# Mixing of two expert outputs on TensorE: diagonal products in place of scale, add and turn

## The reference

```python
scores = jax.nn.softmax(xf @ gate_w.T, axis=-1)
top_v, top_i = jax.lax.top_k(scores, TOP_K)              # TOP_K = 2
top_v = top_v / jnp.sum(top_v, axis=-1, keepdims=True)
for e in range(N_EXPERTS):                               # 8
    w_e = jnp.sum(jnp.where(top_i == e, top_v, 0.0), axis=-1)
    h = _gelu(xf @ fc1_w[e].T + fc1_b[e])
    y = h @ fc2_w[e].T + fc2_b[e]
    out = out + w_e[:, None] * y
shared = _gelu(xf @ w1_w.T + w1_b) * (xf @ w3_w.T + w3_b) @ w2_w.T + w2_b
return (out + shared)                                    # and x + this
```

## Time and profile before

| | us |
|---|---|
| median of 3 runs | 1638.67 |
| lowest and highest of them | 1627.11, 1644.32 |
| the profiled execution, its time | 1633.87 |
| its span in the trace | 1631.9 |
| busy in the span: PE, PEld, DVE, ACT, POOL | 1389.5, 1186.8, 1112.7, 770.3, 415.2 |

### The profile page before, as it was taken

How to read it: one execution, slowest core, us unless ns; L and a number is a source line. 1 busy time by engine, 2 the same in 40 slices (tenths; PEclk the granted TensorE clock), 3 DMA queues, 4 the chain that set the end, 5 groups by cost and what they waited for, 6 DMA issues and landing times. The chain is left out here.

```text
span 1631.9 us, 49725 instructions
## 1 busy us (share of the span) xinstructions
PE 1389.5 (85%) x19283; PEld 1186.8 (73%) x19283; DVE 1112.7 (68%) x3948; ACT 770.3 (47%) x1702; POOL 415.2 (25%) x686
## 2 busy tenths in 40 slices
PE   3858888888887679999995889989998869899998
PEld 3847777777776568778874657768887458777885
DVE  7867777777777864768766693644443774677764
ACT  3733333333334465656633432645555255556651
POOL 2732222222222701000022310356655041000003
PEclk9955555555555789999996579989999579999996
DMA  3000000000000246887966402423222555789865
GB/s 96 1 21 4 4 4 4 4 4 4 4 4 4 88 144 138 248 247 203 177 140 181 135 15 97 151 94 94 87 87 75 153 157 145 180 268 242 184 132 123
DMA packets 73124, 169.05 MB, mean 104 GB/s; under 512 B 18466, under 2 KB 43754, under 8 KB 70396
## 3 DMA queue, kind: packets, MB, share of 16 engines
q1 hardware_dynamic: 67516, 153.03, 35.5%
q0 software_dynamic: 5376, 12.85, 2.6%
HBM read 93.60 MB, written 67.42 MB: 99 GB/s over the span
## 5 line engine op out<-in xcount | busy, mean ns | idle before, releaser
L514 PE MATMUL gru_ps_r<-gru_hp,gru_wp 128*128 128x16 f16 x3920 | 199.7, 176 | 68.3 <-DVE gru_hp L489 68.3
L1375 DVE TENSOR_REDUCE l_mt<-l_ps 98x2 fp32r<-98x392 f32 x384 | 198.8, 560 | 72.7 <-PE l_ps L1139 70.1
L514 PEld LDWEIGHTS gru_ps_r<-gru_hp,gru_wp 128*128 128x128 f16 x3920 | 150.5, 105 | 88.7 <-DVE gru_hp L489 88.7
L1327 ACT ACTIVATE l_arena<-l_ps 98x784 f32<-98x784 f32 x192 | 158.3, 824 | 90.3 <-PE l_ps L1162 87.0
L514 PE MATMUL gru_ps_n<-gru_hp,gru_wp 128*128 128x16 f16 x3920 | 191.2, 174 | 0.0
L580 ACT ACTIVATE gru_reset<-gru_ps_r,gru_unscale 128x32 f32<-128x32 f32 x196 | 56.5, 288 | 216.6 <-PE gru_ps_r L514 216.6
L514 PEld LDWEIGHTS gru_ps_n<-gru_hp,gru_wp 128*128 128x128 f16 x3920 | 150.0, 104 | 0.0
L567 POOL TENSOR_TENSOR gru_kept<-gru_keep,l0s_state 128x32 f32<-128x32 f32 x196 | 49.4, 252 | 305.3 <-ACT gru_keep L582 305.3
L1139 PE MATMUL l_ps<-l_arena,l_arena 128*98 128x196 f32 x768 | 109.2, 262 | 5.8 <-DVE l_arena L1357 2.7
L1139 PEld LDWEIGHTS l_ps<-l_arena,l_arena 128*98 128x98 f32 x768 | 88.6, 166 | 27.4 <-DVE l_mt L1375 20.8
L1162 PE MATMUL l_ps<-l_unit,l_mt 98*98 98x196 f32 x768 | 103.0, 256 | 0.0
(11 more groups left out here) (390 smaller groups left out, 4033.0 us busy)
## 6 DMA issues: line engine op xcount, KB each, us to landing
l_arena<-qk SPq DMA_DIRECT2D x96, 294.0 KB
qk<-l_arena SPq DMA_DIRECT2D x48, 392.0 KB, 6.1
rel<-l_arena SPq DMA_DIRECT2D x24, 686.0 KB
l_arena<-rel SPq DMA_DIRECT2D x48, 343.0 KB
qk<-l_arena SPq DMA_DIRECT2D x12, 784.0 KB, 6.6
l_arena<-in_experts_dram SPq DMA_DIRECT2D x8, 1152.0 KB, 7.7
l_arena<-x SPq DMA_DIRECT2D x24, 294.0 KB, 4.6
l_arena<-l_arena SPq DMA_DIRECT2D x48, 98.0 KB, 3.3
```

The costliest lines, as they stand in the source:

```text
L514: last = pe.matmul(out[:, b, B * m:B * m + B], wp[:, wi, g, m, :], hp[:, b, part, B * k:B * k + B], start=False, stop=True, skip_group_che ...
L1327: act.activation(probs[g % SLOTS][:TH, :, :], banks, ACT.Exp).then_inc(p_ready, 1)
L1375: dve.tensor_reduce(mt[:TH, g % 2, 2 * head:2 * head + 2], ps[:TH, S_BANK + head, :TB].rearrange("p (h k) -> p h k", h=2), AXIS.X, ALU.max ...
```

## The change

For every half the weighted sum and the turn become two products per chunk. The stationary operand is y1 (98 tokens by 128 or 64 channels), the moving one is a 98x98 matrix with w1 on its diagonal, and the same with y2 and w2 adds into the same place of PSUM. Both are float32 in full. DVE builds the diagonals ahead, by 16 products of identity and weight for four halves each. The biases' products come first, for a whole tile of 392 tokens at once, and the four products of each half add to them. Four tiles have homes in PSUM (eight banks) in place of two, and the biases of the first four are computed right after the gates are turned. y1 and y2 have a home for each of the eight pairs, so SP issues all sixteen loads with no wait between, and then stores tile by tile. ACT's scaling and DVE's weighted sum are gone, with ym and their semaphores; `gate_cols` moves up in the arena.

```diff
-    y1, y2 = (arena.place(n * 3 * GROUP * C, 3, GROUP, C) for n in range(2))
-    ym = arena.place(6 * GROUP * C, 2, GROUP, C)
+    y1, y2 = (arena.place(n * NT * GROUP * C, NT, GROUP, C) for n in range(2))
+    diagonals = [arena.place(AT_DIAGONALS + k * N, HALVES, TH) for k in range(2)]
@@ SP
-                for n in range(HALVES // GROUP):
-                    if n >= 3:
-                        sp.wait_ge(mixed, GROUP * (n - 2))
+                for n in range(NT):
                     for k, y in ((0, y1), (1, y2)):
                         first_row = k * N + n * GROUP * TH
-                        sp.dma_start(y[:TH, n % 3, :, :], ...).then_inc(pair_in[n % 3], 16)
-                    if n >= 2:
-                        sp.wait_ge(added, 2 * (n - 1))
-                        ...
+                        sp.dma_start(y[:TH, n, :, :], ...).then_inc(pair_in[n], 16)
+                for n in range(NT):
+                    sp.wait_ge(added, 2 * (n + 1))
+                    ...
@@ PE
+                def bias(n):
+                    for k, (at, width) in enumerate(CHUNKS):
+                        pe.matmul(ps[:width, 2 * (n % 4) + k, :TB], bias_parts[:, at:at + width], gate_cols[:3 * E, n, :],
+                                  start=True, stop=False, skip_group_check=True)
                 pe.wait_ge(bias_ready, 1)
+                for n in range(4):
+                    pe.wait_ge(gates_kept, n + 1 if n < 2 else NT)
+                    bias(n)
                 for n in range(NT):
-                    pe.wait_ge(gates_kept, n + 1)
+                    if n >= 4:
+                        pe.wait_ge(added, 2 * (n - 3))
+                        bias(n)
+                    pe.wait_ge(pair_in[n], 32)
                     for j in range(GROUP):
                         i = n * GROUP + j
-                        pe.wait_ge(mixed, i + 1)
-                        ...                    # turns, wait for them, bias products
+                        if j == 0:
+                            pe.wait_ge(diagonal_ready, 2 * (n + 1))
                         for k, (at, width) in enumerate(CHUNKS):
+                            out = ps[:width, 2 * (n % 4) + k, j * TH:(j + 1) * TH]
+                            pe.matmul(out, y1[:TH, n, j, at:at + width], diagonals[0][:TH, i, :], start=False, stop=False, skip_group_check=True)
+                            last = pe.matmul(out, y2[:TH, n, j, at:at + width], diagonals[1][:TH, i, :], start=False, stop=True, skip_group_check=True)
-                    last.then_inc(biased, 1)
+                    last.then_inc(summed_pairs, 1)
@@ ACT
-                for i in range(HALVES):
-                    ...
-                    act.activation(ym[:TH, n % 2, j, :], y1[:TH, n % 3, j, :], ACT.Copy, scale=w1[:TH, i:i + 1]).then_inc(scaled, 1)
@@ DVE
+                for n in range(NT):
+                    for k, w in ((0, w1), (1, w2)):
+                        of = slice(n * GROUP, (n + 1) * GROUP)
+                        dve.tensor_tensor(diagonals[k][:TH, of, :],
+                                          w[:TH, of].rearrange("p (i a) -> p i a", a=1).to_broadcast([TH, GROUP, TH]),
+                                          ident[:TH, :TH].rearrange("p (a t) -> p a t", a=1).to_broadcast([TH, GROUP, TH]),
+                                          ALU.mult).then_inc(diagonal_ready, 1)
                 dve.wait_ge(xs_in, 32 * NT)
                 for n in range(NT):
-                    for j in range(GROUP):
-                        ...
-                        dve.scalar_tensor_tensor(y, y2[:TH, n % 3, j, :], w2[:TH, i:i + 1], y, ALU.mult, ALU.add).then_inc(mixed, 1)
-                    ...                        # add tile n - 1, moments of tile n - 2
+                    dve.wait_ge(summed_pairs, n + 1)
+                    ...                        # add tile n, moments of tile n - 1
```

More of the change, by code:

```diff
@@ L692 @@
 ARENA = AT_TILES + 26 * TB
+AT_DIAGONALS = 19200
 MAGIC = 1.5 * 2.0 ** 23
@@ L1679, in mixture @@
     yg, yl = arena.place(AT_TILES + 6 * F, OUTS, C), arena.place(at + GATHERS * 256 + 1024, 2, C)
-    gate_cols = arena.place(8 * GROUP * C, NT, TB, dt=f32r)
+    gate_cols = arena.place(2 * NT * GROUP * C, NT, TB, dt=f32r)
     l3_raw, spot = [], E * EXPERT
@@ L1727, in mixture @@
         share_ready, gate_rounded, gates_ready = (s.sem(n) for n in "share_ready gate_rounded gates_ready".split())
-        yl_ready, gates_turned, gates_kept, biased = (s.sem(n) for n in "yl_ready gates_turned gates_kept biased".split())
+        yl_ready, gates_turned, gates_kept = (s.sem(n) for n in "yl_ready gates_turned gates_kept".split())
         w_high, w_low, tail_low = s.sem("w_high"), s.sem("w_low"), s.sem("tail_low")
@@ L1736, in mixture @@
         hgh_ready, hgl_ready, out_summed, yg_ready, tail_ready = (s.sem(n) for n in "hgh_ready hgl_ready out_summed yg_ready tail_ready".split())
-        xs_in, pair_in = s.sem("xs_in"), [s.sem(f"pair_in{n}") for n in range(3)]
-        scaled, mixed, y_turned, added, done = (s.sem(n) for n in "scaled mixed y_turned added done".split())
+        xs_in, pair_in = s.sem("xs_in"), [s.sem(f"pair_in{n}") for n in range(NT)]
+        diagonal_ready, summed_pairs, added, done = (s.sem(n) for n in "diagonal_ready summed_pairs added done".split())
         def down_of(t):
@@ L2250, in _ @@
                 dve.wait_ge(xs_in, 32 * NT)
                 for n in range(NT):
-                    for j in range(GROUP):
-                        i = n * GROUP + j
-                        dve.wait_ge(scaled, i + 1)
-                        y = ym[:TH, n % 2, j, :]
-                        dve.scalar_tensor_tensor(y, y2[:TH, n % 3, j, :], w2[:TH, i:i + 1], y, ALU.mult, ALU.add).then_inc(mixed, 1)
-                    if n >= 1:
-                        c = n - 1
-                        dve.wait_ge(biased, c + 1)
-                        for k, (at, width) in enumerate(CHUNKS):
-                            x = xs[:width, k, c * TB:(c + 1) * TB]
-                            dve.tensor_tensor(x, x, ps[:width, 2 * (c % 2) + k, :TB], ALU.add).then_inc(added, 1)
@@ L2263, in _ @@
-                    if n >= 2:
-                        new_moments.tile(dve, lambda k, cols: xs[:CHUNKS[k][1], k, cols], n - 2, added)
-                c = NT - 1
-                dve.wait_ge(biased, c + 1)
-                for k, (at, width) in enumerate(CHUNKS):
-                    x = xs[:width, k, c * TB:(c + 1) * TB]
-                    dve.tensor_tensor(x, x, ps[:width, 2 * (c % 2) + k, :TB], ALU.add).then_inc(added, 1)
-                for n in (NT - 2, NT - 1):
-                    new_moments.tile(dve, lambda k, cols: xs[:CHUNKS[k][1], k, cols], n, added)
+                    dve.wait_ge(summed_pairs, n + 1)
@@ L2274, in experts_layer @@
+                    for k, (at, width) in enumerate(CHUNKS):
+                        x = xs[:width, k, n * TB:(n + 1) * TB]
+                        dve.tensor_tensor(x, x, ps[:width, 2 * (n % 4) + k, :TB], ALU.add).then_inc(added, 1)
+                    if n >= 1:
+                        new_moments.tile(dve, lambda k, cols: xs[:CHUNKS[k][1], k, cols], n - 1, added)
+                new_moments.tile(dve, lambda k, cols: xs[:CHUNKS[k][1], k, cols], NT - 1, added)
 def experts_layer(nc, ins, x_in, y_out, scratch, moments, ahead, averages):
```

30 lines of the change are left out of this document (6 added, 24 removed).

## The result

The change makes the kernel slower. Its median is 1670.7 us (four executions, 1655.7 to 1677.1) against 1639.6 us for the kernel before (four, 1627.1 to 1644.3); the ratio is 1.0174, 95% interval 1.0127 to 1.0222. The prediction said 1629.0, with 1651.7 for its first rival; the time lies outside its range of 1618 to 1655. (A ratio compares only executions within 1.5% of their kernel's fastest, so it can differ from that of the medians.)

A forecast was written before the change was run, and what follows sets the result against it. It took a PE chain at 1.2 GHz, a third latency, as the bound. A 28.1 us loop from 1266.2 would end at 1294.3 instead of 1304.02: -9.7 us, so 1638.67 becomes 1629.0; range 1618 to 1655.

The forecast's parts named there:

- Rival 1: Granted clock stays at 0.50 through the loop of float32 products: +13.0 us, 1651.7; chance 0.36.
- What bounds the kernel before: Stage's loop is a PE chain at 1.2 GHz, 1.128 us a half, with 32 waits of 0.41 us.
- The clock: In the loop: low at first, rising to 2.4 GHz after some 5 us; loop 28.1 us, change -9.7 us.
- The size of a half: Loop's eight records a half: 4 x 0.213 + 4 x 0.163 = 1.50 us at 1.2 GHz, 0.755 at 2.4.
- the bound from unlike rows: Loop's record spacing: -15.4 us if loads take no more than movement, +5 if loads and movement don't overlap.
- The sum: Halves plus exposed biases: 12.2 us earlier all at 2.4 GHz, 13.0 later all at 1.2; forecast -9.7.
- diagonals: DVE builds 16 diagonals at 0.42 to 0.5 us each, 8 us in all, from 1259.2 to 1267.5.
- the first pair's landing: First pair has landed at 1266.2; PE starts there instead of at 1267.92, gaining 1.7 us at the front.
- VectorE under TensorE: DVE's adds and statistics in the loop take some 2.6 us a tile, under PE's 3.0.
- a tail: From PE's last instruction to the next layer's L204: 5.7 us, no gain taken.
- no gain from the homes: Loads of pairs in the loop before: ACT waits 15.8 us for them, but PE is never late for them.
- nothing waits: Stores queue behind sixteen loads, 7.5 us of issue until 1269.5; the first add comes at 1269.2 or later.

The follow-up runs named there:

- The version with turns and one bias a tile: Kernel before with own homes for all pairs and bias products once a tile behind its four turned halves; stages 41.3 and 40.0 us, medians 1631.0 and 1628.1 us.
- the filled kernel: Changed kernel plus twenty full-shape products that nobody reads, between the gates' turns and the bias products; stage 51.7 us, four executions from 1629.6 to 1671.1 us.
- the order by chunk: Changed kernel with the loop over the chunks outside the halves, so 2 width changes a tile instead of 8; stage 67.7 us, time 1658.1 us.

## Why the prediction was wrong

**What bounds the kernel before** was right: a chain on TensorE, a third of it latency. The version with turns and one bias a tile takes away 24 of the 32 waits and 48 small products, without any diagonal, and gains 9 to 10 us of the stage, 4.5 of it without the own homes.

**The clock** is the step that failed. The prediction took the rise as "likelier, narrowly, after some 5 us"; it never came in 66 us. Rival 1 named the mechanism, with its place. The argument for the rise was that the stream had no waits and more partitions than the mixture of the earlier trace rows. The first half was wrong, as the stalls show, and the second not enough: with 128 partitions, and with few stalls or none, the clock does rise, 7 us into the loop, and the stage is 46.6 to 48.4 us, 2 to 4 under before, where the forecast had 9.7 under. Why the clock is granted or not beyond that stays open.

**The size of a half** failed as well, also in the rival: 1.95 us, not 1.50. Its terms were right: 0.213 and 0.163 us a record stand in the trace wherever the width stays. (The second with some luck: 1.75 ns a column comes from the shorter of the two records of the earlier trace rows, 349 ns. Their median, 359, would have given 2.4 ns and 0.23 us.) Missing was the stall at each change of width. "The new stream has no waits either" was right of semaphores and wrong of the engine. The trace of before changes width in every half too, but in turns, which start 0.17 us apart on both widths (eight in 1.54 us above), and the wait of 0.41 us hid what the bias products might have shown; the bound from unlike rows was the place to be wider. This step alone would have undone the forecast. An estimate with the clock as forecast and the halves as measured: 5 us at 1.2 GHz cover 2.6 halves, the other 29.4 take 32.4 us at 1.10, and the bias products of four tiles 0.55 each, as in the filled kernel (1276.52 to 1277.07). That is 39.6 us, and the end comes at 1305.8, 1.8 us later than before and not 9.7 earlier.

**The sum** closes. Rival 1 gave +13.0 us. The loop is 66.15 us, from 1277.70 to 1343.32 + 0.53. The bias products of tiles 4 to 7 cost 0.95 us a tile (one pair starts at 1308.84, the first product behind it at 1309.79) instead of 0.66: 1.2 us more. What is left, 66.15 - 3.8 over 32, is 1.948 us a half, 0.444 over the sum of its records: the stalls, 14.2 us. The first pair comes 0.3 us later after the first turn, and the tail is 5.29 instead of 5.71. That is +28.3; measured are 28.2. Had the clock been at 1.00 throughout, the stage would be, by an estimate, that of the filled kernel less the 1.9 us by which its loop starts later after the first turn, 49.8 us: the stalls would have left 0.6 of the 12.2 us that the prediction had for that case. From the changed kernel's stage the order by chunk took 11 us and the high clock of the filled kernel 27: the two overlap, as a stall costs less at 2.4 GHz.

**What was right beside it**: diagonals (7.7 us for 8 predicted), the first pair's landing, VectorE under TensorE, a tail of 5.3 for 5.7, no gain from the homes in a loop of that pace. The issue of sixteen loads takes 14.6 us and not 7.5. It holds the first store back by 0.8 us, against the prediction's "nothing waits", but without cost, as the stage ends with the last tile.

**The range** ended at 1655 because the rival's half had no upper bound of its own. With the stalls at the price that they have, rival 1 would have stood at 1666 (1651.7 + 14.2), 5 us under the measured median, which lies within the spread of its executions.

## What to carry over

Give float32 products that follow one another the same number of columns in the load, even at the price of padding: here 128 columns throughout were quicker than 128 and 64 in turn (a stage of 71.7 us against 78.6). When a change swaps a waiting chain for a dense stream of float32 products, price the stream at 1.2 GHz and count on 2.4 only if full-shape products of that very kind show it in a trace. And look first whether the latency can be spread over more work where it stands: one wait and two bias products a tile instead of four and eight gave more than the new scheme in any of its forms, by the stage.

## What was not expected of the hardware

- A change between 128 and 64 loaded columns stalls TensorE by 0.22 us at 1.2 GHz and 0.16 us at 2.4, in float32 products; with the width kept, a change of PSUM bank or region leaves the rows 0.43 us apart. From float32 products of 98 partitions to float32r products of 24, with 128 columns on both sides, the step grows by 0.13 us.
- Turns of 128 and 64 columns in float32 alternate without such a stall: eight in 1.54 us at 1.2 GHz.
- With TensorE busy practically throughout, the granted clock stayed at 0.50 for 60 to 66 us with 98 partitions or with stalls (three kernels, four traces), and rose after 7 us with 128 partitions and 128 columns, or 128 partitions and few stalls (two kernels, three traces). A clock that was at 1.00 ahead of the loop stayed there for 38 us with 98 partitions and stalls.
- Behind twenty filler products the clock was still at 1.00 in the loop with 128 partitions, for 38 us in one kernel and for 1.7 in another; with 24 partitions it fell 0.3 us after them.
- A float32 turn that carries the start flag makes a later product without the flag overwrite columns of its PSUM bank beyond its own 98. The Trainium skill, PSUM — Partial Sum Buffer, The four PSUM rules, says that the flag clears the marks of the whole bank, in the partition groups that are written. The runs agree: with the flag on every turn mixed picks were lost, with the flag on a bank's first turn alone none were. That it is three halves in four follows from the rule, and no run counts them.
